# The first half of a two-expert weighted sum moved from VectorE to GpSimd

## The reference

```
x = layernorm(x + attn(x)); x = layernorm(x + xattn(x, ctx)); x = layernorm(x + ffn(x))
# ffn: of 8 experts each token uses its best 2
out = expert_weights[t, 0] * y[t, expert 0] + expert_weights[t, 1] * y[t, expert 1]   (+ bias)
```

## Time and profile before

| | us |
|---|---|
| median of three runs | 2222.88 |
| the profiled execution, its own time | 2224.16 |
| its span | 2222.4 |
| busy: PE, DVE, ACT, POOL | 1953.6, 1294.2, 999.2, 477.6 |

### The profile page before, as it was taken

The page is one execution under the profiler, slowest core; times in us unless marked ns, Lnnn a source line. Parts: engine busy times, 40 slices in busy tenths (PEclk is TensorE's granted clock), DMA queues, the critical chain, the costliest instruction groups (busy, mean ns, idle before and its releaser), DMA issues. The chain is left out here.

```text
span 2222.4 us, 32846 instructions
## 1 busy us (share of the span) xinstructions
PE 1953.6 (88%) x10990; PEld 1004.1 (45%) x10991; DVE 1294.2 (58%) x2318; ACT 999.2 (45%) x1921; POOL 477.6 (21%) x801
## 2 busy tenths in 40 slices
PE   8699999688669999967999999997887999977992
PEld 4344445333546666643222222253453444464662
DVE  3478784687612222246888888745576887653115
ACT  2156665377211111123466666763542666632331
POOL 2220011522123222212100000023242011033441
PEclk9689999799779999988799999997997999987996
DMA  8522312421730101136211111034225333052223
GB/s 220 137 50 46 62 32 45 101 55 21 278 115 28 33 28 33 28 117 147 34 29 30 30 30 30 2 87 101 46 73 107 59 59 59 2 166 66 63 64 128
DMA packets 111607, 157.90 MB, mean 71 GB/s; under 512 B 31543, under 2 KB 88695, under 8 KB 108535
## 3 DMA queue, kind: packets, MB, share of 16 engines
q1 hardware_dynamic: 103986, 135.75, 26.9%
q0 software_dynamic: 7488, 20.46, 3.0%
HBM read 110.44 MB, written 44.72 MB: 70 GB/s over the span
## 5 line engine op out<-in xcount | busy, mean ns | idle before, releaser
L1598 ACT ACTIVATE arena<-psum 128x512 f32<-128x512 f32 (+1 forms) x1120 | 574.6, 591 | 360.9 <-PE psum L1539 184.2
L1631 DVE TENSOR_REDUCE arena<-psum 128x1 f32<-128x1024 f32 (+3 forms) x352 | 399.9, 1172 | 94.0 <-PE psum L1515 64.9
L1515 PE MATMUL psum<-arena 96*128 96x512 bf16 (+7 forms) x1280 | 366.6, 369 | 31.0 <-DVE arena L1674 12.0
L1539 PE MATMUL psum<-arena 99*128 99x512 bf16 (+7 forms) x1280 | 366.0, 353 | 21.7 <-DMA arena<-arena 13.5
L1617 DVE CUSTOM_DVE_ANT_0 arena<-psum,arena 128x640 bf16<-128x640 f32 (+3 forms) x256 | 250.1, 1022 | 66.6 <-PE psum L1515 65.3
L1557 PE MATMUL psum<-arena 128*32 128x512 f32 (+3 forms) x2560 | 281.5, 538 | 1.1 <-ACT arena L1598 1.1
L2175 PE MATMUL psum<-arena 128*128 x780 | 270.5, 493 | 1.9 <-ACT arena L2229 1.2
L1515 PEld LDWEIGHTS psum<-arena 96*128 96x128 bf16 (+1 forms) x1280 | 100.8, 100 | 272.9 <-issue 82.4
L1539 PEld LDWEIGHTS psum<-arena 99*128 99x128 bf16 (+1 forms) x1280 | 124.6, 99 | 195.9 <-ACT arena L1598 76.4
L2279 DVE COPY arena<-psum 128x640 f32<-128x640 f32 (+1 forms) x78 | 59.3, 760 | 252.6 <-PE psum L2185 252.6
L2194 PE MATMUL psum<-arena 128*128 (+1 forms) x780 | 189.1, 384 | 2.1 <-DVE arena L2282 1.2
(11 more groups left out here) (206 smaller groups left out, 2360.7 us busy)
## 6 DMA issues: line engine op xcount, KB each, us to landing
arena<-k_parts SPq DMA_DIRECT2D x144, 128.0 KB
q_halves<-arena SPq DMA_DIRECT2D x80, 192.0 KB, 3.2
arena<-q_halves SPq DMA_DIRECT2D x40, 384.0 KB, 4.8
arena<-q_halves SPq DMA_DIRECT2D x40, 256.0 KB, 5.2
k_parts<-arena SPq DMA_DIRECT2D x48, 192.0 KB, 3.2
arena<-in_L_ffn_w SPq DMA_DIRECT2D x9, 1024.0 KB, 12.8
arena<-y_rows SPq DMA_DIRECT2D x32, 256.0 KB, 4.1
arena<-in_L_ffn_w SPq DMA_DIRECT2D x8, 704.0 KB, 11.3
```

The lines of the kernel that those rows point to most:

```text
L1515: last = nc.tensor.matmul(dst[:, base + lo:base + hi], q[0:rows, qh, h, qb % 4 * P:qb % 4 * P + P], k[0:rows, h, key0 + lo:key0 + hi], sta ...
L1539: last = nc.tensor.matmul(b[:, at0:at0 + width], kk[0:rows, h, kb * P:kb * P + P], q[0:rows, qh, h, c0:c1], start=True, stop=diag is None)
L1598: nc.scalar.activation(probs[k % 4][:, heads[0]:heads[-1] + 1, c0:c1], bank[st_bank[no % 3]][:, 0:len(heads) * width].rearrange("p (h q) - ...
L1631: nc.vector.tensor_reduce(dst, src, AX.X, ALU.max).then_inc(t("taken"), 1)
```

## The change

In the two comb stages POOL makes gate times row of choice 0 in place in `gathered` (two instructions a pair), waits for that on its own semaphore, and adds `x_tok` into `r_tok` (two instructions), which signals `first_row`. DVE waits for `first_row` instead of the rows and keeps the two instructions of choice 1. POOL waits for the rows and for the norm of pair p - 4 (`xs`). In the plan a POOL task "half" of 2.3 us stands ahead of the add, whose cost falls from 1.9 to 0.95 us.

```diff
                         task("SP", "load", p, 1.0, 5.0 if p < 4 else 3.5, ("add", p - 4))
-                    task("DVE", "add", p, 0.75 if source == "proj" else 1.9, 0.15, ("prj", p), ("load", p),
+                    if source == "comb":
+                        task("POOL", "half", p, 2.3, 0.2, ("load", p), ("norm", p - 4))
+                    task("DVE", "add", p, 0.75 if source == "proj" else 0.95, 0.15, ("prj", p), ("half", p),
                          (normed if not norm else "norm", p - 4), ("more", p - 4))
...
+            def pool_half(pool, p):
+                if p >= 4:
+                    pool.wait_ge(t("xs"), 2 * (p - 4) + 2)
+                pool.wait_ge(t(f"rows{p % 4}"), 32 * (p // 4 + 1))
+                for u in (2 * p, 2 * p + 1):
+                    nc.gpsimd.tensor_scalar(gathered[:, 0, u % TPB, :], gathered[:, 0, u % TPB, :], gate_w[:, 0, u:u + 1],
+                                            None, ALU.mult).then_inc(t("weighted"), 1)
+                for u in (2 * p, 2 * p + 1):
+                    pool.wait_ge(t("weighted"), u + 1)
+                    nc.gpsimd.tensor_tensor(r_tok[:, u % TPB, :], gathered[:, 0, u % TPB, :], x_tok[:, u, :], ALU.add)                        .then_inc(t("first_row"), 1)
...
             def pool_prog(pool):
                 for kind, n in plan.get("POOL", []):
+                    if kind == "half":
+                        pool_half(pool, n)
...
-                dve.wait_ge(t(f"rows{p % 4}"), 32 * (p // 4 + 1))
-                for n in range(2):
-                    for u in (2 * p, 2 * p + 1):
-                        last = nc.vector.scalar_tensor_tensor(
-                            out=r_tok[:, u % TPB, :], in0=gathered[:, n, u % TPB, :], scalar=gate_w[:, n, u:u + 1],
-                            in1=x_tok[:, u, :] if n == 0 else r_tok[:, u % TPB, :], op0=ALU.mult, op1=ALU.add)
-                        if n == 0:
-                            last.then_inc(t("first_row"), 1)
-                    if n == 0:
-                        dve.wait_ge(t("first_row"), 2 * p + 2)
+                dve.wait_ge(t("first_row"), 2 * p + 2)
+                for u in (2 * p, 2 * p + 1):
+                    last = nc.vector.scalar_tensor_tensor(
+                        out=r_tok[:, u % TPB, :], in0=gathered[:, 1, u % TPB, :], scalar=gate_w[:, 1, u:u + 1],
+                        in1=r_tok[:, u % TPB, :], op0=ALU.mult, op1=ALU.add)
                 last.then_inc(t("r"), 1)
```

## The result

The changed kernel took 2225.82 us (median of 20 runs, 2218.75 to 2234.73), the kernel before 2220.34 beside it (20 runs, 2209.72 to 2226.07). The ratio is 1.0027, with a 95% interval of 1.0014 to 1.0040: 6.0 us slower, between 3 and 9 (the two medians lie 5.5 us apart). The profiled execution took 2230.61 us, its span is 2228.9.

What follows compares the result with a forecast made beforehand. DVE was taken to bound t7 and set t3's pace, with PE 2 us behind. t7's +3.8 and t3's -0.3 gave +3.5 us: 2227.7 profiled, 2226.4 against the median runs; range 2216 to 2235.

Steps and rivals of the forecast that it cites:

- t7, +3.8 forecast: Last comb stage, from 2187 us to the end: 32.0 us against 28.2, with DVE and POOL both nearly full.
- The fill: In t7 DVE starts only after POOL's first four instructions, 3.0 us after the rows land.
- The pace: In t7 a pair costs 3.77 us of DVE, 2.64 own work plus 1.1 of shared turns, against 3.52 before.
- rival B: POOL sets the pace in t7; with TENSOR_SCALAR at 1.1 us, +12.3 us in all, 2235; chance 0.2.
- The shared turn: DVE and POOL alternate instructions on SBUF; each shared turn delays DVE by 0.35 or 0.55 us, mean 0.45.
- the tail: In t7 the last pair costs DVE 2.64 us, with no POOL work left beside it.
- t3, -0.3 forecast: Earlier comb stage, about 970.7 to 1045.5 us: a start 1.8 us later less 2.1 from three rounds.
- The start: In t3 POOL's halves of pairs 0 and 1 delay PE's first units by 1.8 us.
- The rounds: In t3 each 14.1 us round of half a batch entry's tokens falls to 13.4, -0.7 each over three rounds.
- rival C: In t3 L894 waits behind POOL's halves, places come free late and PE waits: t3 +4.8, total 2231.5 us; chance 0.12.
- A: POOL's TENSOR_SCALAR costs what COPY does, 0.40 us; most of the 0.88 us a pair is kept: 2216; chance 0.15.
- D: DVE and POOL don't take turns, since the new TENSOR_SCALARs read one tile only: 2218 us; chance 0.08.

Runs made afterwards that it cites:

- e11: The kernel before, with POOL in t7 also running four TENSOR_SCALARs a pair on a tile nobody reads; t7 31.6 us for 28.3, run 2231.48 us.
- e12: The kernel before, with POOL in t7 also running four TENSOR_TENSORs a pair on a tile nobody reads; t7 36.2 us for 28.3, run 2231.84 us.
- e3: The changed kernel with the plan's cost of a half set from 2.3 to 3.3 us; 2224.60 us, ratio to the kernel before 1.0014.
- e6: The changed kernel's written-out order, POOL's halves left out and both halves made by DVE; t3 80.4 us, t7 28.5, one run 2220.26 us.
- e4: The changed kernel with POOL helping only pairs 2 to 7 of t3 and 1 to 6 of t7, plan cost 3.3; 2226.28 us, ratio 1.0017.
- e5: The changed kernel with other engines in the order of the kernel before, halves put into POOL's list; t3 77.6 us, t7 31.7, one run 2225.79 us.
- e8: The changed kernel with POOL helping only pairs 2, 3 of t3 and 1, 3, 5, 7 of t7, plan cost 3.3; 2225.07 us, ratio 1.0025.
- e9: The changed kernel with SP's loads for the next stage moved behind all of t3's stores; t3 73.2 us, one run 2229.13 us.

## Why the prediction was right, and where its steps were wrong

It forecast +3.5 us and a time of 2226.4; measured were +6.0 (3 to 9) and 2225.82. That the time came within 0.6 us is luck: the three runs that it started from had a median of 2222.88, the kernel before took 2220.34 beside the changed one, 2.5 us less, and the change cost 2.5 us more than forecast. By stages, t7 came out as forecast through errors that cancelled, and t3 did not come out at all.

- **t7, +3.8 forecast, +3.9 in the profile.** The fill held. The pace did not: I had DVE full, with its own 2.64 us and 1.1 of turns a pair, and POOL nearly so. POOL alone is full (23.43 of 23.50 us), and DVE is idle for a quarter of that stretch, which is rival B's mechanism. The terms were 3.0 + 7 x 3.77 + 2.64 = 32.0; they came as 3.3 + 23.5 + 5.5 = 32.3. Three errors cancelled. TENSOR_SCALAR was priced at 0.82 us from L1733 and takes 0.93 (TENSOR_TENSOR 0.69, two of them in 1.39 undisturbed, for 0.63), so POOL's half is 3.24 us. The shared turn was priced too high: a pair costs 3.35 and not 3.77. And the tail, one pair in the sum, is about twice that.
- **The turn.** I took the 1.23 us of a turn beside a 512-column TENSOR_TENSOR in the earlier trace rows and subtracted the same 0.2 for both kinds of instruction. e11 and e12 show that the kinds differ: 0.10 us of DVE's time for each TENSOR_SCALAR and 0.25 for each TENSOR_TENSOR, where my 0.55 and 0.35 a turn, at 2.5 turns for four instructions, make 0.34 and 0.22. The second was about right and the first three times too high. L894 has two inputs, so it was the wrong neighbour for a TENSOR_SCALAR. The Trainium skill ("SBUF — State Buffer", Who interferes with whom) says that the loser is held for the whole instruction; e11 does not bear that out for a one-input instruction of POOL, which takes 0.93 us: the longest sum beside it took 0.70 us for 0.48, and the mean cost was 0.10.
- **The tail.** "The written-out order of all engines is searched anew ... I put 2 us on that" was the step that was too small. In t7 the order cost 1.6 us (e3); in t3, with all of DVE's old work, 5.6 (e6).
- **t3, -0.3 forecast, +5.6 in the profile.** The start was 3.1 us later where I said 1.8, since a half takes 3.24 us and pair 1's waits for pair 0's. The rounds gave back 3.2 where I said 2.1: they came to 11.4 to 11.7 us, not 13.4. So up to PE's last stretch the sum was right: it begins 0.1 us earlier than before, for 0.3. But e4 has no late start and is no shorter. The failed step is that I balanced DVE against PE by rounds and took the end of the stage as PE's own work that could only start earlier. It is not: it hangs on when half 1's stores land, because `ahead` and then half 2's stores stand behind them on SP's queue, and half 3's units need the places. The row for it was in my hands, ACT's 3.85 us in the earlier trace rows; I used it for rival C alone. The runs show in its place a start 3.0 us later behind the late stores and 2.6 us at the lower clock, which no term held.
- **Rivals.** A fell (0.93 us, not 0.40). The rule of the Trainium skill behind it ("GPSIMD Engine Reference", Engine selection), one-input work at roughly line rate on GpSimd, does not hold for this TENSOR_SCALAR: 0.93 us beside DVE's 0.44 for the same columns and more arithmetic. B was right in kind, POOL paced t7, at half its price. C named the right wait, a place that comes free late, and came nearest in size for t3 (+4.8). Its cause, POOL's halves, makes the place late under the old order (e5, ACT waits 5.55 us), but it is not the only one: e6 has no halves on POOL and ACT waits 6.78 us. D fell: the one-input instruction does hold DVE, only less.

Not settled: what makes half 1's stores late in the changed kernel, the order, the blocked sums at adds 4 and 5, or the late start. Four different orders (after, e3, e4, e8) gave 80 to 82 us, and the old one 74 to 75 without POOL's halves and 77.6 with them. Nor was it separated how much of e5's 2.8 us is the start and how much is blocking. Shown is the common end: late stores behind `ahead`, a place that comes free late, an idle PE, and in all but e5 the lower clock.

## What to carry to other kernels

An engine that helps another must beat the old pace by enough to pay for the fill and the tail. Here a pair costs 3.35 us on POOL against 3.52 on DVE alone, a gain of 0.17, and fill and tail cost 3.3 and 2.0 us: by an estimate from these figures it would take some 30 pairs to break even, and a stage has 8. When the order of a kernel comes from a search over estimated costs, an edit of one cost reorders everything; test the new order with the old instructions, as e6 does, and the new instructions under the old order, as e5 does, before laying a loss to either. And at the end of a stage look at the queue with transfers of two kinds: what waits behind the bulk loads for the next stage may set this one's end.

## What the runs showed of the hardware

- TENSOR_SCALAR on POOL with its scalar from a tile, 128x256 f32: 0.93 us (median), TENSOR_TENSOR 0.69 to 0.72. From L1733 at 128 columns and L899 at 2, TENSOR_SCALAR had come out at 0.82.
- Beside it, DVE loses 0.10 us to a TENSOR_SCALAR and 0.25 to a TENSOR_TENSOR of POOL, averaged over t7's mix of instructions (e11, e12). BATCH_NORM_STATS2 keeps its 0.41 us a piece in both.
- POOL's closing DRAIN ends 6.45 us after POOL's last instruction in every profile where POOL works in t7 (e3: 2209.20 to 2215.66), so work given to POOL at the very end of a kernel can end the execution by itself (e11).
- After 4.25 us of idling PE's granted clock was 0.50, and eight matmul records took 6.48 us for 3.91; after 2.80 us (e5) it was 1.00 and they took 3.70; without the idling (e9) sixteen took 7.27. So of t3's 5.6 us about 2.6 are the clock and 3.0 the later start.
